# Attention on one core: queries take over the keys' projection, the last layer takes over the values', and GpSimd splits the keys

## The reference

```
xd      = (layernorm(x) @ W_down).reshape(b, t, 16, 16)
keys    = einsum('bthk,hik->bthi', xd, tokeys)    * 16 ** -0.25
queries = einsum('bthk,hik->bthi', xd, toqueries) * 16 ** -0.25
values  = einsum('bthk,hik->bthi', xd, tovalues)
attn    = softmax(einsum('bqhs,bkhs->bhqk', queries, keys))
out     = einsum('bhqk,bkhs->bqhs', attn, values).reshape(b, t, 256) @ W_unify + b_unify
x       = x + out
```

## Time and profile before

| | |
|---|---|
| median of 3 runs | 2948.91 us (2944.68 to 2953.52) |
| profiled execution, its own time | 2942.43 us |
| its span | 2940.3 us |
| PE busy | 2753.6 us (94%) |
| PE weight loads busy | 1663.3 us (57%) |
| DVE busy | 2133.7 us (73%) |
| ACT busy | 1863.4 us (63%) |
| POOL busy | 539.7 us (18%) |
| DMA traffic | 180.69 MB |

### The profile page before, as it was taken

One profiled execution on the slowest core, in us unless ns is written; L12 is line 12 of the kernel. 1 busy time (PEld: TensorE's weight loads), 2 busy tenths in 40 slices (PEclk: granted clock), 3 DMA queues, 4 the chain that ended last, 5 costly groups with the idle time before them and its releaser, 6 DMA issues. The chain is left out here.

```text
span 2940.3 us, 49181 instructions
## 1 busy us (share of the span) xinstructions
PE 2753.6 (94%) x17263; PEld 1663.3 (57%) x17263; DVE 2133.7 (73%) x3460; ACT 1863.4 (63%) x3505; POOL 539.7 (18%) x498
## 2 busy tenths in 40 slices
PE   5999999867999999999999999999999679999997
PEld 3799998853334343333343443333433369999886
DVE  6554456748888888898898888888897465445664
ACT  5444455634777777777777777777777454544564
POOL 3354124520000000000000000000000145421353
PEclk9999999977999999999999999999999889999998
DMA  5221113415033132131230330321220412111242
GB/s 170 65 57 43 43 59 113 130 38 89 15 58 69 25 65 47 38 60 36 48 73 15 59 67 23 67 45 37 47 43 8 149 47 72 52 48 43 89 140 66
DMA packets 159668, 180.69 MB, mean 61 GB/s; under 512 B 31816, under 2 KB 129296, under 8 KB 159504
## 3 DMA queue, kind: packets, MB, share of 16 engines
q1 hardware_dynamic: 151312, 167.99, 23.4%
q0 software_dynamic: 8192, 10.57, 1.2%
HBM read 96.46 MB, written 30.49 MB: 43 GB/s over the span
## 5 line engine op out<-in xcount | busy, mean ns | idle before, releaser
L1518 DVE TENSOR_REDUCE at_mxc<-at_pb 128x2 f32<-128x1024 f32 x1024 | 1222.7, 1219 | 159.6 <-PE at_pb L1335 152.0
L1448 ACT ACTIVATE at_ex<-at_pd 128x512 f32<-128x512 f32 x2048 | 1092.9, 598 | 355.0 <-PE at_pd L1346 346.4
L768 DVE TENSOR_TENSOR f_ml_hl<-f_ml_h,f_ml_hh 128x512 fp32r<-128x512 f32 (+1 forms) x384 | 265.2, 692 | 441.1 <-ACT f_ml_hh L844 382.8
L1346 PE MATMUL at_pd<-at_qa,at_ka 50*128 50x512 f32 x2048 | 573.4, 466 | 3.3 <-ACT at_ex L1448 2.5
L1346 PEld LDWEIGHTS at_pd<-at_qa,at_ka 50*128 50x128 f32 x2048 | 255.8, 185 | 526.9 <-issue 271.3
L1355 PE MATMUL at_po<-at_ex,at_va 128*32 128x512 f32 x4096 | 547.1, 606 | 0.2 <-ACT at_ex L1448 0.2
L841 ACT ACTIVATE f_ml_h<-f_ml_pL,b1T 128x512 f32<-128x512 f32 (+1 forms) x384 | 243.6, 634 | 449.9 <-PE f_ml_pL L895 373.6
L1335 PE MATMUL at_pb<-at_ka,at_qa 48*128 48x512 f32 x2048 | 441.8, 450 | 16.0 <-DVE at_mxc L1518 10.7
L910 PE MATMUL f_ml_pA<-f_wh,f_ml_hh 128*128 128x256 f32 (+1 forms) x1408 | 408.8, 290 | 0.0
L912 PE MATMUL f_ml_pA<-f_wl,f_ml_hh 128*128 128x256 f32 (+1 forms) x1408 | 401.3, 285 | 0.0
L913 PE MATMUL f_ml_pA<-f_wh,f_ml_hl 128*128 128x256 f32 (+1 forms) x1408 | 401.3, 285 | 0.0
(11 more groups left out here) (124 smaller groups left out, 2658.9 us busy)
## 6 DMA issues: line engine op xcount, KB each, us to landing
f_wraw<-in_L_ffn_w SPq DMA_DIRECT2D x128, 256.0 KB, 2.7
at_qa<-at_parts SPq DMA_DIRECT2D x384, 64.0 KB, 2.4
at_ka<-at_parts SPq DMA_DIRECT2D x384, 64.0 KB, 2.4
f_ro_xr<-in_L_attn_x SPq DMA_DIRECT2D x16, 512.0 KB, 3.6
f_ml_xr<-in_L_attn_x SPq DMA_DIRECT2D x16, 512.0 KB, 3.9
x<-f_ml_yo SPq DMA_DIRECT2D x16, 512.0 KB, 3.8
at_xr<-x SPq DMA_DIRECT2D x16, 512.0 KB, 5.2
at_xres<-x SPq DMA_DIRECT2D x8, 1024.0 KB, 6.6
```

The lines of the kernel that those rows point to most:

```text
L768: eng.tensor_tensor(hl[h % RING][:, 0:w], h32[h % 2][:, 0:w], hh[h % RING][:, 0:w].bitcast(F32), ALU.subtract).then_inc(s_lo.sem, 1)
L1346: eng.matmul(pd[n % RING][:, :], ka[g][rows, p, kt * P:(kt + 1) * P], qa[g][rows, qh, p, :], start=True, stop=True).then_inc(s_full.sem, 1)
L1448: eng.activation(ex[t % 2][:, j, :], pd[n % RING][:, :], ACT.Exp).then_inc(s_free[n % RING].sem, 1)
L1518: eng.tensor_reduce(mxc[:, t // NT, kh, t % NT::NT], pb[kh][:, :].rearrange("p (e k) -> p e k", e=2), AX.X, ALU.max).then_inc(s_mx.sem, 1)
```

## The change

Scores need only the product of queries and keys. The change multiplies, once, the queries' matrix with the keys' matrix of each block, and uses the result (`qk`) for the queries with the whole scale, while the keys are the rows xd themselves. Likewise the values' matrix is multiplied once into W_unify (`wu` is overwritten), and the values are xd, transposed. The four key products of a batch leave the table; POOL makes the high part and the rest of the keys from xd in SBUF (`key_parts`), 2 instructions for each of the 4 xd tiles of a batch. SP's head load waits for them as well (`s_kp`). The order of XD is now c outside and f inside. The semaphore `s_row` is folded into `s_xl`.

```
     def turn_step(self, eng):
-        for q in range(3 * DT):
-            eng.wait_ge(self.s_diag, q + 1)
-            mm = eng.transpose(self.place(q), self.diag[:, q, :, :].rearrange("p h s -> p (h s)"), self.k.ident[:, :])
+        eng.wait_ge(self.s_diag, 3 * DT)
+        for c in range(DT):
+            eng.matmul(self.bank[:, c * P:(c + 1) * P], self.block(0, c), self.block(1, c), start=True, stop=True)
+        for c in range(DT):
+            mm = eng.matmul(self.bank[:, 512 + c * D:512 + (c + 1) * D], self.block(2, c), self.w.wu[:, c, :],
+                            start=True, stop=True)
         mm.then_inc(self.s_turned, 1)
     def copy_step(self, eng):
         eng.wait_ge(self.s_turned, 1)
-        for q in range(3 * DT):
-            ins = eng.tensor_copy(self.w.bd[:, q // DT, q % DT, :], self.place(q))
-        ins.then_inc(self.s_diag, 1)
+        eng.tensor_copy(self.w.qk[:, :, :], self.bank[:, 0:DT * P].rearrange("p (c i) -> p c i", c=DT))
+        eng.tensor_copy(self.w.wu[:, :, :],
+                        self.bank[:, 512:512 + DT * D].rearrange("p (c d) -> p c d", c=DT)).then_inc(self.s_diag, 1)
...
-        XD = [("xd", c, f) for f in range(2) for c in range(DT)]
-        QK = [("qk", m, c, f) for c in range(DT) for m in range(2) for f in range(2)]
+        XD = [("xd", c, f) for c in range(DT) for f in range(2)]
+        QK = [("qk", c, f) for c in range(DT) for f in range(2)]
...
             if g == 1 and not last:
-                table.update(zip((2, 3, 5, 6, 7, 8, 10, 11, 13, 14), XD[-2:] + QK))
+                table.update(zip((2, 3, 5, 6, 7, 8), XD[-2:] + QK))
...
-                sides = [self.place(task, 0, 0, 0) for task in XT + XD + QK[:4] + V + QK[4:]]
+                sides = [self.place(task, 0, 0, 0) for task in XT + XD + QK[:2] + V + QK[2:]]
...
                 if j == 0:
                     eng.wait_ge(s_free[n % RING].sem, s_free[n % RING].at(ring.freed(n)))
+                    eng.wait_ge(s_kp.sem, s_kp.at(2 * len(XD) * b + len(XD) * (c + 1)))
...
                 elif a.kind == "qk":
-                    m, c, f = a.at
-                    mm = eng.matmul(bank[:, :], w.bd[:, m, c, :], xd[:, c, f * 512:(f + 1) * 512], start=True, stop=True)
+                    c, f = a.at
+                    mm = eng.matmul(bank[:, :], w.qk[:, c, :], xd[:, c, f * 512:(f + 1) * 512], start=True, stop=True)
                 elif a.kind == "v":
                     for i in range(2):
                         tile = 2 * a.at[0] + i
                         for c in range(DT):
-                            mm = eng.matmul(bank[:, i * D + c * P:i * D + (c + 1) * P], xd[:, c, tile * P:(tile + 1) * P],
-                                            w.bd[:, 2, c, :], start=True, stop=True)
+                            mm = eng.transpose(bank[:, i * D + c * P:i * D + (c + 1) * P],
+                                               xd[:, c, tile * P:(tile + 1) * P], k.ident[:, :])
...
+            def key_parts(ring, a):
+                c, f = a.at
+                at = slice(f * 512, (f + 1) * 512)
+                n = 2 * (len(XD) * a.b + 2 * c + f)
+                eng.wait_ge(s_free[a.n % RING].sem, s_free[a.n % RING].at(ring.freed(a.n)))
+                if f == 0:
+                    for two in s_ld[2 * c:2 * c + 2]:
+                        for s in two:
+                            eng.wait_ge(s.sem, s.at(16 * ULOADS * a.b))
+                eng.tensor_copy(parts[:, 1, 0, c, at], xd[:, c, at]).then_inc(s_kp.sem, 1)
+                eng.wait_ge(s_kp.sem, s_kp.at(n + 1))
+                eng.tensor_tensor(parts[:, 1, 1, c, at], xd[:, c, at], parts[:, 1, 0, c, at].bitcast(F32),
+                                  ALU.subtract).then_inc(s_kp.sem, 1)
```

More of the change, by code:

```diff
@@ L1019, in spread_step, with block @@
                               self.mask, ALU.mult).then_inc(self.s_diag, 1)
[L1021 to L1022 removed]
+    def block(self, m, c):
+        return self.diag[:, m * DT + c, :, :].rearrange("p h s -> p (h s)")
     def turn_step(self, eng):
[L1025 to L1027 removed]
+        eng.wait_ge(self.s_diag, 3 * DT)
[4 more added lines that the diff above has]
+                            start=True, stop=True)
         mm.then_inc(self.s_turned, 1)
@@ L1110, in attention @@
         s_hi = S("s_hi")
+        s_kp = S("s_kp")
         s_ld = [[S(f"s_ld{g}{p}") for p in range(2)] for g in range(4)]
@@ L1256, in ones @@
                         to = t[r0:r0 + MROWS, :, :].rearrange("r a (x q) -> r (a x) q", q=P)
-                        eng.dma_start(to.bitcast(F32), row).then_inc(s_row, 16)
+                        eng.dma_start(to.bitcast(F32), row).then_inc(s_xl.sem, 16)
             def load_maxima(ring, a):
@@ L1302, in step @@
                         load_maxima(self.ring, a)
-                    if a and (a.kind, *a.at) in (QK[3], QK[7]):
-                        self.parts_in[b + 1, a.at[1]] = a.n
+                    if a and (a.kind, *a.at) in (QK[1], QK[3]):
+                        self.parts_in[b + 1, a.at[0]] = a.n
                     if (g, t) in HEAD_AT:
@@ L1460, in side_out @@
                                 eng.wait_ge(s.sem, s.at(16 * ULOADS * a.b))
-                    eng.activation(parts[:, m, 0, c, f * 512:(f + 1) * 512], bank[:, :], ACT.Copy,
-                                   scale=SCALE).then_inc(s_hi.sem, 1)
+                    eng.activation(parts[:, 0, 0, c, f * 512:(f + 1) * 512], bank[:, :], ACT.Copy,
+                                   scale=SCALE * SCALE).then_inc(s_hi.sem, 1)
                     return
@@ L1548, in side_out @@
                 if a.kind == "qk":
-                    m, c, f = a.at
+                    c, f = a.at
                     at = slice(f * 512, (f + 1) * 512)
                     eng.wait_ge(s_hi.sem, s_hi.at(a.ns + 1))
-                    ins = eng.scalar_tensor_tensor(parts[:, m, 1, c, at], bank[:, :], SCALE,
-                                                   parts[:, m, 0, c, at].bitcast(F32), ALU.mult, ALU.subtract)
+                    ins = eng.scalar_tensor_tensor(parts[:, 0, 1, c, at], bank[:, :], SCALE * SCALE,
+                                                   parts[:, 0, 0, c, at].bitcast(F32), ALU.mult, ALU.subtract)
                 elif a.kind == "mx":
@@ L1631, in _ @@
             s_xb.open(eng)
+            s_kp.open(eng)
             diagonals.mask_step(eng)
+            def key_parts(ring, a):
+                c, f = a.at
+                at = slice(f * 512, (f + 1) * 512)
+                n = 2 * (len(XD) * a.b + 2 * c + f)
+                eng.wait_ge(s_free[a.n % RING].sem, s_free[a.n % RING].at(ring.freed(a.n)))
+                if f == 0:
+                    for two in s_ld[2 * c:2 * c + 2]:
[5 more added lines that the diff above has]
+                                  ALU.subtract).then_inc(s_kp.sem, 1)
             class Do:
@@ L1636, in before @@
                         norm.pow_step(eng, f, 4)
+                    for a in sides:
+                        if a.kind == "xd":
+                            key_parts(self.ring, a)
                 def first(self, a):
@@ L1646, in step @@
                         norm.pow_step(eng, 2 * (b + 1) + t // 4, 4)
+                    if a and a.kind == "xd":
+                        key_parts(self.ring, a)
                     if g == 2 and t == 8:
-                        eng.wait_ge(s_xl.sem, s_xl.at(16 * (b + 1)))
+                        eng.wait_ge(s_xl.sem, s_xl.at(16 * (8 + b + 1)))
                         for q in range(0, NT, 2):
```

11 lines of the change are left out of this document (4 added, 7 removed).

## The result

| | before | after |
|---|---|---|
| median | 2947.43 us (4 runs, 2944.68 to 2953.52) | 2909.55 us (4 runs, 2906.08 to 2913.04) |
| profiled execution, its own time | 2942.43 us | 2909.2 us |
| its span | 2940.3 us | 2907.5 us |

The ratio of after to before is 0.9874 (95% interval 0.9859 to 0.9889), so the change makes the kernel 1.3% faster. In a later set of runs the same pair gave 0.9892 (0.9875 to 0.9908): 2940.35 and 2909.39 us. The forecast was 2916 us, and for the profiled execution 2909.9 us.

What follows compares the result with a forecast made beforehand. PE was taken as the bound in the mean, DVE near, so step lengths priced the change: 21.8 + 9.0 + 1.7 = 32.5 us off 2948.9 gives 2916 us, range 2908 to 2927.

Steps and rivals of the forecast that it cites:

- The keys: Steps 10, 11, 13 and 14 of unit 1 lose their key products: 0.78 us a step, 21.8 us in all.
- rival A: The emptied steps stay at a light side step's 3.10 us: keys give 8.1 us, total 2930 us; chance 5%.
- The values: Loop's v steps: 4 transposes replace 8 product instructions, 3.42 to 3.10 us a step, 9.0 us in all.
- POOL: Key parts in the loop: 8 instructions of 1.26 us, 10.1 us a batch, costing zero since nothing waits soon.
- POOL beside DVE: Joining of the maxima, step 3 of unit 1, held by POOL: taken as zero, at most 7 us.
- The opening: SP's first head load and the chain behind it come 1.7 us earlier; between zero and 2 us possible.
- C: Maxima beside key parts, units 0 and 1: each POOL instruction costs DVE 1.0 us, slower, 2972 us; chance 3%.
- D: PE's clock falls in the transposing steps, 4.06 us instead of 2.61: slower, 2957 us; chance 2%.

Runs made afterwards that it cites:

- The keys' run alone: The kernel after with the values' part undone, v again by products against the values' matrix: 0.9911 of the kernel before, 2928.63 us.
- the halved maxima: The kernel after with each of DVE's maxima taken over half of the columns: 2903.54 us (one run), batch 196.56 us.
- the run alone: The kernel before with only the values' part of the change, keys and queries as before: 0.9966, 2941.99 against 2953.38 us.
- the doubled transposes: The kernel after with each of v's transposes done twice, 8 in a v step: 2921.49 us (one run), v steps of 3.35 us.
- The late key parts: The kernel after with three more POOL additions of 128x512 ahead of each tile's key parts: 2919.42 us (one run), batch 197.39 us.

## Why the prediction was right

**The keys: right.** 0.78 us a step was forecast and measured (3.39 to 2.61), 21.8 us in the loop. The keys' run alone gave 3.17 us a batch, 22.2 us. Reading the floor from a step that stood empty already was the step that carried it; rival A, that DVE keeps these steps at 3.10 us, is refuted twice, by the result and, as far as DVE goes, by the halved maxima. What the prediction did not say is why the floor is 2.61 us: it read the length from the trace, and only the experiments show the ring of banks behind it.

**The values: right, slightly low.** 0.32 us a step and 9.0 us were forecast; the steps gave 0.33 us, and the run alone 1.53 us a batch, 10.7 us in the loop. Its mechanism was told incompletely: I took the length from a step of the same shape, which is correct, and the doubled transposes show that this length is not PE's work alone; the fourth score product's wait for the second exponential shows that it is the ring of banks.

**POOL: covered, as forecast.** The subtraction took 1.26 to 1.28 us. The copy took 0.61 us and lies outside the range that I gave, 0.82 to 1.26: the memset of a quarter of the size, times four, is no lower bound. Nothing hung on it. The late key parts show how much cover there is: 6.5 us more of POOL per pair of tiles, nothing lost in the loop.

**POOL beside DVE: the hold right, the reason for the zero wrong.** I took zero for the joined maxima, since the instruction is short and would have to meet one of POOL's, with 7 us as the upper end. It met one in each of the seven batches prepared in the loop, and was held by 0.79 us. It costs 0.01 us in its step, because the wait for a bank behind it is longer. So the zero came true by luck: nothing in the prediction knew of that slack. The Trainium skill's statement (GPSIMD Reference, Specifications) on contention for VectorE instructions with two SBUF inputs agrees with this row, 0.176 to 0.965 us; that the instruction is held only when it begins while POOL's is running, and then ends with it, is shown by the timelines here and not by the page. POOL's one-input copy never met a joining, so this is shown for its additions and subtractions alone.

**The opening: right in place, short in size.** 1.7 us were forecast, with 2 us as the most, and 2.45 came. 1.97 us are there at SP's first load; the rest appears between that load and the first maximum product (10.59 us before, 10.12 after), and its cause stays open. POOL's key parts were in time by 3.6 us.

**The slower rivals.** C (POOL holds DVE's maxima): excluded by 1024 maxima of at most 1231 ns even with 512 POOL instructions added. D (the clock): excluded for groups of four and of eight transposes. The rule of the Trainium skill (TensorE: Matmul & The Clock Gate, Part 4) that transposes don't count as busy in the same way has no effect here, where products of other kinds stand around them; a stretch of nothing but transposes was not tried.

**The total.** 32.5 us were forecast; 32.8 us came in the profiled spans, 37.9 and 31.0 us between the medians in two sets of runs. The loop is where the match means something (30.8 forecast, 31.05 measured). That the profiled pair agrees to 0.3 us is partly luck, since the opening gave 0.75 us too much and the feed-forward layers took 0.7 us back.

## What to carry to other kernels

Where a loop repeats to the nanosecond, price an edit by step lengths, taken from steps that already look like the edited one, and not from busy shares: DVE at 88% and PE at 99% both looked like the bound, and in the empty steps neither was. Count the tiles that pass through a ring of PSUM banks in one step: the next cost is the round trip of a bank (here four or five tiles for three banks), and a small product can cost as much as a larger one if it holds a bank at the wrong moment (0.27 and 0.66 us of PE both make a step of 3.10 us), so try it first in its step, with its input ready. Work on data that lies in SBUF can go to an idle POOL nearly free, as long as the DVE instructions beside it read PSUM, as the maxima do here.

## What was not expected of the hardware

- POOL's copy of 128x512 float32 into fp32r took 0.611 us (0.611 to 0.616, 32 of them), less than half of its two-input subtraction (1.263 to 1.287).
- A DVE instruction of 16 columns with both inputs in SBUF that begins while a POOL addition or subtraction runs ends about 30 ns behind the end of that one: 0.51 to 0.96 us in place of 0.176 (7 in the kernel after, 35 with more POOL work). If it begins 0.1 us ahead of POOL's, it isn't held (22 cases). DVE's reductions from PSUM aren't held at all (1024, at most 1231 ns).
- Eight transposes of 128 columns in float32 take about as long as eight instructions of the float32 product (1.09 and 1.16 us). A float32 product of 128 columns is two instructions in the profile, a transpose one, and that is most of the saving (0.26 of 0.33 us a step).
